# Second stage of a transformer kernel: expert groups of two batches and a shorter lag, in place of four and four

## The reference

```
x = x + attention_16_heads(context, layernorm(x))
x = x + mixture(layernorm(x))
x = x + attention_1_head(layernorm(x), context, context, mask)
x = x + routed_ffn(layernorm(x))
```

```
gate   = x @ gate_w.T + gate_b                       # picks two experts a token
counts = how often each expert was picked, over all 32 batches
out    = sum over e of  relu(x @ expert_w[e].T + expert_b[e]) * counts[e] / total
```

```
logits = q @ context.T / 16 + mask * (-1e9)
out    = softmax(logits) @ context
```

## Time and profile before

| | |
|---|---|
| time, median of 3 runs | 985.68 us (983.68 to 988.55) |
| the profiled execution | 987.03 us, span 984.9 us |
| busy share of the span | PE 91%, DVE 74%, ACT 55%, POOL 56% |
| second stage | from 461 to about 775 us |
| mean granted clock of PE | 0.958 of full speed |

### The profile page before, as it was taken

The page is one execution under the profiler, slowest core; times in us unless marked ns, Lnnn a source line. Parts: engine busy times, 40 slices in busy tenths (PEclk is TensorE's granted clock), DMA queues, the critical chain, the costliest instruction groups (busy, mean ns, idle before and its releaser), DMA issues. The chain is left out here.

```text
span 984.9 us, 31478 instructions
## 1 busy us (share of the span) xinstructions
PE 900.4 (91%) x10664; PEld 668.7 (68%) x10664; DVE 730.3 (74%) x2071; ACT 543.4 (55%) x1068; POOL 551.4 (56%) x897
## 2 busy tenths in 40 slices
PE   4799999999999999986999999999976399999993
PEld 2477777777777777754466666666644289889892
DVE  6688888888888888866778888888865356666773
ACT  3377777777777777654044444444443065555551
POOL 6655555565555555401037777777776535556536
PEclk9899999999999999987999999999996599999997
DMA  5644554445444454331565555665552348786535
GB/s 157 178 128 142 144 147 134 135 144 147 125 139 141 142 142 144 94 105 47 141 179 174 183 186 186 189 191 184 175 190 90 120 100 197 176 187 105 96 64 59
DMA packets 107278, 140.56 MB, mean 143 GB/s; under 512 B 23929, under 2 KB 92592, under 8 KB 106928
## 3 DMA queue, kind: packets, MB, share of 16 engines
q1 hardware_dynamic: 94594, 121.38, 41.3%
q0 software_dynamic: 12528, 17.18, 9.7%
HBM read 93.38 MB, written 38.35 MB: 134 GB/s over the span
## 5 line engine op out<-in xcount | busy, mean ns | idle before, releaser
L999 DVE TENSOR_REDUCE smax<-psum 112x2 f32<-112x750 f32 x240 | 216.3, 933 | 24.5 <-PE psum L439 24.4
L840 ACT ACTIVATE probsT<-psum 125x896 f32<-125x896 f32 x173 | 158.7, 917 | 22.0 <-PE psum L454 20.6
L2035 POOL DMA_INDIRECT out_dram<-y,token_at x63 | 101.6, 1612 | 93.9 <-DMA out_dram<-y,token_at 42.2
L1733 DVE SCALAR_TENSOR_TENSOR acc<-psum,neg_bias,acc 128x448 f32<-128x448 f32 x112 | 75.9, 680 | 10.9 <-PE psum L1556 9.3
L1475 POOL DMA_INDIRECT dispatch_dram<-rows,slots_at x64 | 64.0, 1000 | 28.4 <-issue 28.4
L439 PE MATMUL psum<-k_stack,q_stack 63*128 63x375 f16 x480 | 69.3, 326 | 3.9 <-DVE smax L999 2.8
L1556 PE MATMUL psum<-xT_hi,we_hi 128*128 128x448 f16 x256 | 70.2, 356 | 1.1 <-ACT we_hi L1655 1.1
L476 PE MATMUL psum<-probsT,v_aug 125*32 125x112 f32 x2688 | 70.2, 260 | 0.1
L1556 PE MATMUL psum<-xT_lo,we_hi 128*128 128x448 f16 x256 | 69.8, 355 | 0.0
L1556 PE MATMUL psum<-xT_hi,we_lo 128*128 128x448 f16 x256 | 69.7, 354 | 0.0
L476 PEld LDWEIGHTS psum<-probsT,v_aug 125*32 125x32 f32 x2688 | 63.5, 110 | 8.9 <-ACT v_aug L866 8.5
(11 more groups left out here) (298 smaller groups left out, 2448.3 us busy)
## 6 DMA issues: line engine op xcount, KB each, us to landing
k_stack<-k_hi_dram SPq DMA_DIRECT2D x64, 188.0 KB, 2.8
we<-in_ctxT_dram SPq DMA_DIRECT2D x32, 375.0 KB, 3.5
ctxT<-in_ctxT_dram SPq DMA_DIRECT2D x32, 375.0 KB
ctx_rows<-in_ctx_dram SPq DMA_DIRECT2D x32, 375.0 KB
w_raw<-in_w_dram SPq DMA_DIRECT2D x32, 256.0 KB, 3.9
rows_e<-dispatch_dram SPq DMA_DIRECT2D x24, 272.0 KB
k_hi_dram<-k_hi SPq DMA_DIRECT2D x32, 188.0 KB, 2.8
k_lo_dram<-k_lo SPq DMA_DIRECT2D x32, 188.0 KB, 2.7
```

Source lines behind the costliest of these rows:

```text
L840: nc.scalar.activation(probsT[:, p, c, hg, :, :, :].rearrange("p k h q -> p k (h q)"), psum[0:KC, 0:2, 0:4 * S], ACT.Exp, scale=float(HD) ...
L999: nc.vector.reduce_max(smax[:, (u - LAG_B) % 2, 2 * (s % 4) + s // 4::PAIRS], psum[0:S, pair_bank(s):pair_bank(s) + 2, 0:KV], AX.X).then_i ...
L1733: nc.vector.scalar_tensor_tensor(out, psum[:, mix_bank(t, u, k), 0:GT], neg_bias[:, hc, e:e + 1], out, ALU.max, ALU.add).then_inc(m["acc_r ...
L2035: nc.gpsimd.indirect_dma_start(dram["out"], bass.IndirectOffsetOnAxis(token_at[:, unit // PAIR % TOKEN_TURNS, unit % PAIR:unit % PAIR + 1] ...
```

## The change

GB becomes 2 (224 columns a group), and the lags become GB, GB + 1, GB + 2, GB + 3: 2, 3, 4 and 5. A step then does PER_STEP = 8 units of 224 columns (four experts), and a group takes two steps. Two units, the halves `hc` of one expert, share a bank and fill it like one unit before; PE waits for a free bank once per pair, and DVE waits until the pair is complete. On PE and DVE the pair k takes the place of unit k in the step's order, with one exception: in the first step of a group (even u), PE does the pair 0 ahead of accT. On DVE the residual add that needs accT stays ahead of pair 0. The splits of the experts' low halves, spread over three steps before, come in the first two steps. There are 32 steps with mixture and 5 behind them; the first two have mixture alone, and the first two of the last five still have `a`.

```diff
-GB = 4
+GB = 2
...
-    LAG_ATT, LAG_OUT, LAG_ROUTE, LAG_SEND = 4, 5, 6, 7
-    TURN = 2 * GB
+    LAG_ATT, LAG_OUT, LAG_ROUTE, LAG_SEND = GB, GB + 1, GB + 2, GB + 3
+    TURN = 8
+    PER_STEP = E * DC // GB
...
     def mix_bank(t, u, k):
 
-        return MIX_BANKS[(4 * (t * TURN + u) + k) % len(MIX_BANKS)]
+        return MIX_BANKS[(PER_STEP * (t * TURN + u) + k) // DC % len(MIX_BANKS)]
+
+    def mix_unit(u, k):
+
+        return E // GB * (u % GB) + k // DC, k % DC
...
             def mixture(t, u, k):
 
-                e, hc = 2 * (u % GB) + k // 2, k % 2
-                g0 = t * (2 * GT) + (u // GB) * GT
+                e, hc = mix_unit(u, k)
+                g0 = (t * TURN + u) // GB * GT
...
-                wait(pe, m["acc_rdy"], cnt(t, u, 4, k + 1 - len(MIX_BANKS)))
+                if hc == 0:
+                    wait(pe, m["acc_rdy"], cnt(t, u, PER_STEP, k + DC - DC * len(MIX_BANKS)))
...
-                        last = nc.tensor.matmul(psum[:, mix_bank(t, u, k), 0:GT], w[:, kc, e, hc * 128:(hc + 1) * 128], x[:, kc, bass.ds(g0, GT)],
+                        last = nc.tensor.matmul(psum[:, mix_bank(t, u, k), hc * GT:(hc + 1) * GT], w[:, kc, e, hc * 128:(hc + 1) * 128], x[:, kc, bass.ds(g0, GT)],
...
+                if u % GB == 0:
+                    mix(0)
+                    mix(1)
                 if a:
 
-                    wait(pe, m["acc_rdy"], cnt(t, (ua // GB) * GB, 4, 4 * GB))
+                    wait(pe, m["acc_rdy"], cnt(t, (ua // GB) * GB, PER_STEP, PER_STEP * GB))
...
-                mix(0)
-                mix(1)
+                if u % GB > 0:
+                    mix(0)
+                    mix(1)
+                mix(2)
+                mix(3)
                 if o:
...
-                mix(2)
+                mix(4)
+                mix(5)
...
-                mix(3)
+                mix(6)
+                mix(7)
...
             def mix(t, u, k):
-                e, hc = 2 * (u % GB) + k // 2, k % 2
-                out = acc[:, u // GB, hc, :]
-                if isinstance(t, int) and t == 0 and k % 2 == 0 and SPLIT_FIRST + 2 * u + k // 2 < E:
-                    split_expert(SPLIT_FIRST + 2 * u + k // 2)
-                wait(dve, m["ffn_done"], cnt(t, u, 4, k + 1))
+                e, hc = mix_unit(u, k)
+                out = acc[:, u // GB % 2, hc, :]
+                if isinstance(t, int) and t == 0 and hc == 0 and u < GB and SPLIT_FIRST + e < E:
+                    split_expert(SPLIT_FIRST + e)
+                wait(dve, m["ffn_done"], cnt(t, u, PER_STEP, k - hc + DC))
```

More of the change, by code:

```diff
@@ L1721, in mix @@
             def mix(t, u, k):
-                e, hc = 2 * (u % GB) + k // 2, k % 2
-                out = acc[:, u // GB, hc, :]
-                if isinstance(t, int) and t == 0 and k % 2 == 0 and SPLIT_FIRST + 2 * u + k // 2 < E:
-                    split_expert(SPLIT_FIRST + 2 * u + k // 2)
-                wait(dve, m["ffn_done"], cnt(t, u, 4, k + 1))
+                e, hc = mix_unit(u, k)
[3 more added lines that the diff above has]
+                wait(dve, m["ffn_done"], cnt(t, u, PER_STEP, k - hc + DC))
                 if e == 0:
                     wait(dve, m["accT_done"], cnt(t, u - GB - 1, 1, 1))
-                    nc.vector.tensor_scalar(out, psum[:, mix_bank(t, u, k), 0:GT], neg_bias[:, hc, 0:1], bias_sum[:, hc:hc + 1],
+                    nc.vector.tensor_scalar(out, psum[:, mix_bank(t, u, k), hc * GT:(hc + 1) * GT], neg_bias[:, hc, 0:1], bias_sum[:, hc:hc + 1],
                                             ALU.max, ALU.add).then_inc(m["acc_rdy"], 1)
                 else:
-                    wait(dve, m["acc_rdy"], cnt(t, u, 4, k - 1))
-                    nc.vector.scalar_tensor_tensor(out, psum[:, mix_bank(t, u, k), 0:GT], neg_bias[:, hc, e:e + 1], out,
+                    wait(dve, m["acc_rdy"], cnt(t, u, PER_STEP, k - 1))
+                    nc.vector.scalar_tensor_tensor(out, psum[:, mix_bank(t, u, k), hc * GT:(hc + 1) * GT], neg_bias[:, hc, e:e + 1], out,
                                                    ALU.max, ALU.add).then_inc(m["acc_rdy"], 1)
@@ L1770, in step @@
                     mix(t, u, 0)
+                    mix(t, u, 1)
                 if r:
@@ L1789, in step @@
                 if f:
-                    mix(t, u, 1)
+                    mix(t, u, 2)
+                    mix(t, u, 3)
                 if k:
@@ L1799, in step @@
                 if f:
-                    mix(t, u, 2)
+                    mix(t, u, 4)
+                    mix(t, u, 5)
                 if k:
@@ L1824, in step @@
                 if f:
-                    mix(t, u, 3)
+                    mix(t, u, 6)
+                    mix(t, u, 7)
                 if r:
```

## The result

The changed kernel takes 1009.61 us (median of 4 runs, 1006.3 to 1011.37) against 986.68 before (4 runs, 983.68 to 988.55) on the same chip: ratio 1.0224, 95% interval 1.0202 to 1.0246. Forecast were 997.7 and at most 1008: the direction is right, the size only half. The profiled execution was the fastest of the four: 1006.3 us, span 1004.2, which is 19.3 over the profile of before where the forecast's sum was 12.05.

The account below looks back on a forecast made before the run. PE was taken to bound the steady steps at 8.49 us, with DVE next. Steps 1.4, matmuls 2.0, later accT 8.5 and start 0.15 sum to 12.05 us on 985.68, so 997.7 us; range 989 to 1008.

Parts of the forecast that it names:

- accT a pair later in even steps: Even steps 6 to 30: x_res waits for accT, DVE idles 0.84, PE waits 0.65 at route; +8.5 us.
- PE sets the odd step again and DVE gives the lag back: Odd steady steps: DVE has the last pair's turn ready at 6.62, before PE hands it over; no loss, lag doesn't pile up.
- Rival C: DVE binds in both kinds of step at 0.48 a unit: 24.8 in place of 8.5, 1014 us; chance 0.10.
- PE's matmuls: Each mixture step: 24 matmuls of 448 columns become 48 of 224 at 0.096; 0.07 a step, +2.0 us.
- The start: Stage's start: x2n held by the weight piece, PE idles 8 us, then a clock dip; +0.15 us.
- rival B: Start not held: x2n's transposes come at 479.1, 8.8 us less, 988.9 us; chance 0.08.
- Steps: Stage's step count: two more steps at 8.49 (16.98), two attention-only drain steps fewer (15.59); +1.4 us.

Follow-up runs that it names:

- the DMAs apart: Changed kernel with a small unused POOL instruction between the two indirect DMAs of a step, 0.6 us apart: 1002.6 us; with accT first as well 994.4 us.
- accT first: Changed kernel with accT ahead of pair 0 in even steps too: 999.05 us, ratio to before 1.0109.
- the early loads: SP's loads of the first two batches put ahead of its small loads, clears and padding stores; with accT first and the DMAs apart: 991.87 us.
- experiment 7: Changed kernel with SP's loads of the first two batches ahead of its small loads, clears and padding stores: 1000.38 us; with accT first and the DMAs apart 991.87 us.
- experiment 6: Kernel before, its last mixture unit made 0.38 us longer so ends fall behind the second DMA's start: 995.79 us; further runs moved SP's store and ctx_rows load.

## Why the prediction was wrong

Read along one row of runs, the loss of 22.9 us (1009.6 to 986.7) comes apart: the DMAs apart take 7.0 (1002.6), accT first 8.2 more (994.4), the early loads 2.5 more (991.9), and some 5 stay. Each of these is a difference of medians of 2 to 10 runs from several chips. By the ratios, each to the kernel before beside it, the same row reads 5.3, 7.4, 4.1 and 5.2, and an interval of 0.4% to either side is 4 us. The order matters too: accT first by itself takes 10.6 (999.05), and the DMAs apart after it 4.7. So the steps in the traces say more than these times.

- **accT a pair later in even steps: right.** Forecast +8.5, measured 8.2; that they are so close is luck. In the profile DVE idles 0.66 to 1.13 ahead of x_res, 1.05 in the mean, and 0.73 with the DMAs apart (forecast 0.84); route waits 0.48 (forecast 0.65); even steps 9.29 (forecast 9.21), and with the DMAs apart they are 0.64 over the odd ones (9.25 and 8.61; forecast 0.65). The Trainium skill's fixed cost per instruction ("VectorE: DVE Perf Modes", section "The TRN2 errata — SBUF-src ops pay a fixed extra latency per instruction") gave, as an estimate, 358 ns from start to start at 224 columns and a wait of 0.55; measured are 0.37 and 0.48, so rule and row do about equally well here.
- **"PE sets the odd step again and DVE gives the lag back": the step that failed.** The working held for DVE's load: in the odd step shown at first DVE is free for the last pair at 6.64 from accT's start (forecast 6.62) and PE ends that pair at 6.83 (forecast 6.87); in the kernel with the DMAs apart odd steps are 8.61 and wait for nothing. What failed is the hand-over, which the working put at PE's own end with nothing added: DVE takes the pair up at 7.50, and ACT the transposes at 8.22. Odd steps came at 9.16 and not 8.56: 13 x 0.60 = 7.8 us, of which 0.55 each go with the second DMA. With these the forecast's sum is 19.9, beside 19.3 between the two profiles. Rival C had the right place (odd steps wait for xT_lo as well) and the wrong price: DVE's units weren't slower.
- **PE's matmuls: right.** A matmul of 224 columns starts 0.096 behind the one before it, as forecast; with nothing in the way a step is 8.58 (forecast 8.56). The factors as printed give 0.05 a step and 1.4 us, not 0.07 and 2.0; unrounded they give 0.08, and the steps came out 0.09 longer than 8.49.
- **The start: right** as a sum (+0.44 against +0.15): the weight piece holds it. What rival B says of a start that isn't held was tried in experiment 7: its 479.1 for the transposes was right (479.06), its price of 8.8 wasn't (4.5 left at the first route).
- **Steps: right.** The drain lost the two steps it was to lose; behind the last mixture step the profile shows 18.0 us less (forecast 15.6).

Could it have been foreseen? In the trace of before the second DMA starts 0.27 us behind the end of unit 3 and 0.07 behind that of x3nT, in almost every step, so that a shift by one to three tenths of a microsecond brings them together; that could have been read. But nothing on those rows shows a hold, and the same overlap without small groups makes none that a step feels (experiment 6), so its size could not be worked out.

## What to carry to other kernels

When a step is full on one engine and almost full on the next, look not only at the work but at how soon each end is told: idle of an engine whose releaser had ended 0.5 us before is a row of its own, and it shows up by comparing the releaser's end with the waiter's start. Splitting work into half-size pieces cost 0.09 us a step in work here and 0.4 to 0.6 in such delays. In this kernel it helped to keep POOL's second transfer 0.6 us off the last short chain of the step (8.97 to 8.58 a step).

## What the runs showed of the hardware

- In the kernels with groups of two, nearly all ends of PE's work that fell up to 0.35 us behind the start of POOL's second indirect DMA were told at about 0.75 us behind it, some x3 transposes only at 1.45 (0.5 to 1.2 us late); so were a few ends up to 0.25 ahead of it. Not every end near that DMA is: in even steps of the changed kernel s1's end, 0.53 behind it, was signalled 0.014 behind its end. In groups of four, ends 0.1 and 0.3 behind it were told at once (0.04), but for two signals of the ranks (0.35 and 0.32 late).
- Halving the number of PE's signals left the delay as it was, and moving SP's store and its load away from there, one at a time, didn't remove it.
- The delay seems to keep itself up: with accT first x_res starts 0.04 behind accT's end and not up to 0.35 as with the DMAs apart, POOL's DMAs come 0.25 earlier in the step, and the second one again starts ahead of PE's ends. That fits steps of 8.6 and 9.0 in one run.
- A DVE instruction of 0.16 to 0.22 us took 1.0 to 1.9 where POOL's `w_lo` ran beside it, and ended 0.03 to 0.04 us behind it.
